# Adding the residual in the output transfer: a sandwich layer on eight cores whose last addition moves from VectorE into an accumulating DMA

## The reference, cut to what matters

```
x = x + _layernorm(_L0_attn_ref(_layernorm(x)))        # attention, relu scores, no softmax
x = x + _layernorm(_L0_ffn_ref(_layernorm(x)))         # feed-forward

# _L0_ffn_ref, xf = x reshaped to rows of 2048, INTER = 5632
g = einsum('th,ih->ti', xf, gate_w) * gate_s
u = einsum('th,ih->ti', xf, up_w) * up_s
out = einsum('ti,hi->th', silu(g) * u, down_w) * down_s
```

## Time and profile before

| what | value |
|---|---|
| profiled execution, its own time | 1351.65 us |
| span of its slowest core (core 2), first to last instruction | 1350.1 us |
| time around that span | 1.55 us |
| spans of the 8 cores | 1343.7 to 1350.1 us |
| TensorE busy on core 2 | 1138.8 us, 84% of the span |
| VectorE, ScalarE, GpSimd busy | 368.5, 200.8, 46.8 us |
| device memory read and written by core 2 | 170.48 MB, 16.78 MB |
| last matmul to the end of the span | 1294.0 to 1350.1 us |

### The profile page before, as it was taken

The page is one execution under the profiler, slowest core; times in us unless marked ns, Lnnn a source line. Parts: engine busy times, 40 slices in busy tenths (PEclk is TensorE's granted clock), DMA queues, the critical chain, the costliest instruction groups (busy, mean ns, idle before and its releaser), DMA issues. The chain is left out here.

```text
span 1350.1 us, 12668 instructions; the slowest of 8 cores (1343.7 to 1350.1 us)
## 1 busy us (share of the span) xinstructions
PE 1138.8 (84%) x5134; PEld 506.4 (38%) x5236; DVE 368.5 (27%) x406; ACT 200.8 (15%) x255; POOL 46.8 (3%) x68
## 2 busy tenths in 40 slices
PE   2429889870699999999999999999999999999930
PEld 0104334330344444444444444444444444444410
DVE  2057353348400123001230102301023010230385
ACT  2402333242510000000000000000000000000045
POOL 1000000000100000000000000000000000000000
PEclk9859999995599999999999999999999999999975
DMA  6870000006895330943309433094330933302058
GB/s 119 218 156 1 1 1 0 1 1 249 141 172 93 63 63 1 160 90 63 63 1 164 85 63 63 4 169 77 63 63 8 170 72 65 61 8 56 0 158 339
DMA packets 28744, 112.83 MB, mean 84 GB/s; under 512 B 2448, under 2 KB 5008, under 8 KB 24208
## 3 DMA queue, kind: packets, MB, share of 16 engines
q0 software_dynamic: 22784, 75.24, 33.2%
q1 hardware_dynamic: 4752, 33.59, 6.9%
q10 hardware_dynamic: 1152, 3.20, 0.9%
HBM read 170.48 MB, written 16.78 MB: 139 GB/s over the span
## 5 line engine op out<-in xcount | busy, mean ns | idle before, releaser
L736 PE MATMUL ps_f<-lnfT,gw_sb 128*128 128x512 bf16 x1380 | 311.5, 381 | 6.7 <-PEq L74 5.3
L788 PE MATMUL ps_f<-dwb,hdn 128*128 128x512 bf16 x1379 | 303.3, 379 | 12.9 <-DVE hdn L766 11.4
L752 PE MATMUL ps_f<-lnfT,uw_sb 128*128 128x512 bf16 x1380 | 309.1, 379 | 1.5
L766 DVE SCALAR_TENSOR_TENSOR hdn<-ps_f,us_sb,sg 128x1024 bf16<-128x1024 f32 x44 | 56.5, 1284 | 555.1 <-PE ps_f L752 555.1
L788 PEld LDWEIGHTS ps_f<-dwb,hdn 128*128 128x128 bf16 x1408 | 137.4, 98 | 178.9 <-issue 14.1
L736 PEld LDWEIGHTS ps_f<-lnfT,gw_sb 128*128 128x128 bf16 x1408 | 138.3, 98 | 172.9 <-issue 8.4
L752 PEld LDWEIGHTS ps_f<-lnfT,uw_sb 128*128 128x128 bf16 x1408 | 137.8, 98 | 166.1
L762 ACT ACTIVATE sg<-ps_f,gs_sb 128x1024 bf16<-128x1024 f32 x44 | 49.0, 1114 | 831.4 <-PE ps_f L736 831.3
L424 PE MATMUL ps_t<-att,xTb 128*128 128x512 bf16 x500 | 115.8, 386 | 37.4 <-DMA xTb<-xT 36.4
L801 DVE TENSOR_TENSOR acc<-acc,ps_f 128x2048 f32<-128x2048 f32 x40 | 91.5, 2288 | 172.1 <-PE ps_f L788 172.1
L424 PEld LDWEIGHTS ps_t<-att,xTb 128*128 128x128 bf16 x512 | 50.1, 99 | 99.9 <-issue 43.0
(11 more groups left out here) (103 smaller groups left out, 336.8 us busy)
## 6 DMA issues: line engine op xcount, KB each, us to landing
gw_sb<-gw POOLq DMA_DIRECT2D x22, 1024.0 KB, 8.2
uw_sb<-uw POOLq DMA_DIRECT2D x22, 1024.0 KB, 8.7
dwb<-dw POOLq DMA_DIRECT2D x11, 2048.0 KB, 20.3
xbuf<-x SPq DMA_DIRECT2D x8, 1024.0 KB, 22.4
x1sp<-xbuf SPq DMA_DIRECT2D x8, 1024.0 KB, 4.0
x1rb<-x1sp SPq DMA_DIRECT2D x8, 1024.0 KB, 16.5
y<-acc SPq DMA_DIRECT2D x8, 1024.0 KB, 6.3
xTb<-xT POOLq DMA_DIRECT2D x4, 1024.0 KB, 44.4
```

The lines of the kernel that those rows point to most:

```text
L736: e.matmul(ps_f[:, half, :], gw_sb[:, slot, ht * P:(ht + 1) * P], lnfT[:, ht, half * 512:(half + 1) * 512], start=(ht == 0), stop=(ht == H ...
L752: e.matmul(ps_f[:, 2 + half, :], uw_sb[:, slot, ht * P:(ht + 1) * P], lnfT[:, ht, half * 512:(half + 1) * 512], start=(ht == 0), stop=(ht ...
L766: pl.vop(lambda e, gi=gi, li=li: e.scalar_tensor_tensor(hdn[:, li, :], ps_f[:, 2:4, :], us_sb[:, gi:gi + 1], sg[:, gi % 2, :], ALU.mult, A ...
L788: e.matmul(ps_f[:, bs + hc, :], hdn[:, li, tt * P:(tt + 1) * P], dwb[:, li, hc * 512:(hc + 1) * 512], start=(li == 0), stop=(li == blk - 1)),
```

## The change

Three things. The store of x1 at the end of block 2 goes to the output tensor `y` itself, and the scratch tensor is gone. The 8 loads of x1 in the tail, their buffer `x1rb`, and the 8 VectorE additions are gone. The output transfer becomes an accumulating one: the DMA adds its source in `acc` to what `y` holds. It is issued by POOL and not by SP, waits for ScalarE's normalised tile (`sAC`) and for the stores of x1 (`sSP`). In the new kernel the helper `dma` issues the accumulating transfers at its L67, the plain ones at L69.

```
--- before.py
+++ after.py
@@ -62,7 +62,10 @@
         return self.em("scalar", fn, w=list(w) + [("sAC", self.cnt["sAC"])],
                        inc="sAC")
 
-    def dma(self, sem, q, out, in_, w=()):
+    def dma(self, sem, q, out, in_, w=(), accum=False):
+        if accum:
+            return self.em(q, lambda e, o=out, i=in_: e.dma_start(
+                o, i, accum_op=ALU.add), w=w, inc=sem, n=16)
         return self.em(q, lambda e, o=out, i=in_: e.dma_start(o, i), w=w,
                        inc=sem, n=16)
 
@@ -114,7 +117,6 @@
     t_us = nc.dram_tensor("usc", [P, IT], F32, kind="ExternalInput")
     t_ds = nc.dram_tensor("dsr", [P, D], F32, kind="ExternalInput")
     t_y = nc.dram_tensor("y", [R, D], F32, kind="ExternalOutput")
-    t_sp = nc.dram_tensor("x1sp", [R, D], F32, kind="Internal")
 
     es = ExitStack()
     sems = {s: es.enter_context(nc.semaphore(s)) for s in SEMS}
@@ -575,7 +577,7 @@
                 ALU.mult, ALU.mult, accum_out=s2acc[:, dt:dt + 1]), w=w_)
             last_tmpn[0] = ("sDV", pl.v("sDV"))
         sp_done.append(pl.dma("sSP", "sync",
-                              t_sp.ap()[dt * P:(dt + 1) * P, :],
+                              t_y.ap()[dt * P:(dt + 1) * P, :],
                               xbuf[:, dt, :], w=[("sDV", x1_done[dt])]))
     x1sq_ac = pl.v("sAC")
 
@@ -811,18 +813,9 @@
     sTl.close()
 
     s3 = ExitStack()
-    x1rb = s3.enter_context(nc.sbuf_tensor("x1rb", [P, DT, D], F32))
     w1f = s3.enter_context(nc.sbuf_tensor("w1f", [P, DT, D], F32))
 
     pl.new_block()
-    for tt in range(4):
-        pl.dma("sRL", "sync", x1rb[:, tt, :],
-               t_sp.ap()[tt * P:(tt + 1) * P, :], w=[("sSP", SP)])
-    RL1 = pl.v("sRL")
-    for tt in range(4, DT):
-        pl.dma("sRL2", "sync", x1rb[:, tt, :],
-               t_sp.ap()[tt * P:(tt + 1) * P, :])
-    RL2 = pl.v("sRL2")
     out_dma = []
     w1v = {}
     for tt in range(DT):
@@ -862,13 +855,10 @@
             scale=rW8[:, tt:tt + 1], bias=ngW8[:, tt:tt + 1]),
             w=[("sDV", ngw_done)])
         w2v = pl.v("sAC")
-        wfin = [("sAC", w2v), ("sRL", RL1) if tt < 4 else ("sRL2", RL2)]
-        pl.vop(lambda e, tt=tt: e.tensor_tensor(
-            acc[:, tt, :], x1rb[:, tt, :], acc[:, tt, :], ALU.add), w=wfin)
-        fin = pl.v("sDV")
-        out_dma.append(pl.dma("sOUT", "sync",
+        out_dma.append(pl.dma("sOUT", "gpsimd",
                               t_y.ap()[tt * P:(tt + 1) * P, :],
-                              acc[:, tt, :], w=[("sDV", fin)]))
+                              acc[:, tt, :],
+                              w=[("sAC", w2v), ("sSP", SP)], accum=True))
     pl.em("sync", fn=None, w=[("sOUT", out_dma[-1])])
 
     pl.emit(nc, sems)
```

## The result

The changed kernel takes 1379.84 us (median of 9 runs) against 1350.68 us for the kernel before (10 runs): a ratio of 1.0214, 95% interval [1.0204, 1.0225], so 29 us or 2.1% slower. Forecast were 1377.0 us and 1.9%. The profiled execution took 1379.45 us, of which its slowest core, now core 7, spans 1377.9 us.

What follows compares the result with a forecast made beforehand. TensorE bounds until its last matmul, then DMA transfers bound the output stage. First tile at 1323.3, +0.4 issue, +52.0 transfers end the span at 1375.7 against 1350.1; forecast 1377.0 us, range 1363 to 1396.

Steps and rivals of the forecast that it cites:

- (a): Tail: the 8 loads of x1 are hidden behind VectorE's and ScalarE's statistics, so removing them is worth 0.
- (b): Output start: of the 8 removed VectorE additions only the first is on the path, bringing the output 2.6 us forward.
- (d): Output issue: POOL takes 0.76 us per transfer against SP's 0.33; only the first counts, +0.4 us.
- (c): End of block 2: storing x1 to y instead of the scratch tensor moves the same bytes from the same queue, cost 0.
- (e): Output stage: accumulating stores also read 8.39 MB of y, taking 52 us from first issue to end, against 24.2.
- an engine figure and a memory figure: Output stage: 51.8 us by the converting loads' rate, 50 us by device memory's read then write, taken as independent.
- The last term of the sum: Output stage: +27.8 us for a second read in a stage already at the engines' limit.
- the 40.6 us, a rival of the prediction: Output stage: only the engines' read side counts, at its uncontended rate; time 1367.6 us, chance 0.12.
- the estimate of 47 us: Output stage: the skill's read-side rule, 1.93 times the stage's 24.2 us, instead of 52.
- The rival of an absorbed read: Output stage: the second read hides in idle DMA time, stage stays 24.2 us, time 1349.1 us; chance 0.05.
- The rival of poor pipelining: Output stage: each row's write waits for both reads, 61 to 76 us, time 1386 to 1401; 0.26 including slow issue.
- A sign that was forecast wrong: Profile after: device memory totals stay at 170.48 and 16.78 MB, as the read of x1 only moves into the accumulation.

## Why the prediction was right, and where not

- **What bounds the stage: right.** Transfers and not VectorE set the end. Plain stores from POOL with no additions gain 1.9 us and no more.
- **(a) The loads are worth 0: right**, ratio 1.0002 when they alone are gone.
- **(b) The first addition, -2.6 us, and (d) POOL's issue, +0.4: near enough.** Together -2.2 forecast; the run without accumulation is 1.9 us faster, with an interval of about 0.3 to 3.5 us. In detail (d) is about +1.1 and not +0.4: POOL's first issue starts 0.64 us after the tile is ready and lasts 0.90 us, where SP's started 0.09 us after VectorE's tile and took 0.33.
- **(c) The stores of x1 into `y`: nothing seen**; they land in 4.0 us as they did into the scratch tensor.
- **(e) The second read: right that it is paid in full, size 3 us short.** The stage took 55.2 us from first issue to the end, forecast 52.0. The tiles' bytes at the measured 160 GB/s are 52.4 us, as the estimate from the converting loads, 162 GB/s, had it; what was missing is latency and start-up, which I had let the 52 contain: core 7 writes nothing in the first 1.3 us of the stage, 66 GB/s in the next 2.0 and 26 GB/s in the last 1.9. From 1370 to 1376, with core 6 finishing, it wrote 193 GB/s and made up for some of it. The slowest core happened to have its first tile ready 1.3 us earlier than in the profile before, which brought the end within 2.2 us of the forecast. That part is luck.
- **Which limit it is: left open by the prediction, and I first settled it wrongly.** The prediction let an engine figure and a memory figure meet at 52 and called them independent. They are not: the converting load's 162 GB/s is a rate in company, and the same loads run at 210 GB/s once the neighbour is done. So the earlier trace rows did not show an engine's own price, and 51.8 and 50 agree because both are the limit of a pair of cores and not because two limits meet. The last term of the sum speaks of a stage "already at the engines' limit"; it was at the limit of the pair: core 2's plain stores ran at 354 GB/s in company and at 426 from 1345.5 to 1347.5, with core 3 finished, both at a share of about 1. The engines' own limit is the 40.6 us, a rival of the prediction; the sum in SBUF showed it at work (423 GB/s read), the bf16 source showed that it does not bind here.
- **The rule of the Trainium skill** (Collectives: The Full Stack, part 3, on why ReduceScatter is half of AllGather) says that the add is free and the read side pays. The run with the sum in SBUF agrees (423 GB/s read), and so do the 209 and 273 GB/s of cores whose neighbour has finished. In company the read side is not what binds, and the estimate of 47 us was too low. The neighbour was already in the 24.2 us that it multiplied: 47 us is what 16.78 MB take at the 357 GB/s of stores, but accumulation got 320 GB/s of accesses. Why reads and writes together get less than stores alone is open.
- **The rival of an absorbed read** (not slower) would have needed 3.3 us a tile; measured were some 6.6 us. The rival of poor pipelining is refuted by the stage's 55.2 us, below its 61, and by the same traffic in plain transfers, which takes 54.1 us.
- **A sign that was forecast wrong:** device memory read was to stay at 170.48 MB. The page says 162.09, exactly the 8.39 MB of the loads less. With plain stores from POOL, which read nothing at their destination, it says the same 162.09, and with separate plain loads 170.48 again. So this counter leaves out the read that an accumulating transfer makes at its destination, and cannot be used to weigh one.

## What to carry to other kernels

An accumulating store saves an engine's addition and a buffer, but it moves the read of the old value into the output stage; where that stage is already held by transfers, it costs the full time of that read. Weigh a transfer against two limits, the bytes its engines read and the accesses at the memory that neighbour cores share, and take the larger; a busy share near 1 does not say which it is, while the rate after the neighbour has finished does. Here a stage bound by transfers got shorter by starting all of it earlier, or by fewer accesses at the limit that binds; starting only its first piece earlier, or halving the source's bytes at the other limit, gained nothing.

## What the runs showed of the hardware

- The engines of a core read about 404 to 426 GB/s whatever the mix of copy, conversion and addition, where nothing else bound them: 413 and 426 (plain stores), 2 x 202 (converting loads), 2 x 209 (accumulation), 423 (the sum in SBUF). With both neighbour cores at it, each got 320 (accumulation), 324 to 346 (converting loads), 331 (loads and stores) and 357 GB/s (stores) of accesses at the memory.
- A float32 addition in a transfer cost the engines nothing beyond its second read (423 GB/s read in the run with the sum in SBUF), and a bf16 source made it a quarter cheaper for them (273 against 209 GB/s written), which shows only with the neighbour idle.
- The read at an accumulating transfer's destination is missing from the device memory read total, 8.39 MB here.
- POOL needed 0.55 us to issue a plain store of 128 rows of 8 KB, and 0.85 us for an accumulating one.
